# Gates of a GRU and an LSTM loop: input part seeded into PSUM, gates read one by one by ScalarE

## The reference, cut to what matters

```python
# GRU-like layer (h starts from cond_1024)
fused = sigmoid(concat([x_t, h]) @ w_W + w_b)
hidden_state, output_state = split(fused, 2)
memory_state = x_t @ wx_W + wx_b + hidden_state * (h @ wh_W + wh_b)
h_new = output_state * h + (1.0 - output_state) * tanh(memory_state)

# LSTM layer (c starts from 0, h from cond_1024)
a = (x_t @ Wx + b) + h @ Wh            # four parts i, f, o, g
next_c = sigmoid(f) * c + sigmoid(i) * tanh(g)
next_h = sigmoid(o) * tanh(next_c)
```

## Time and profile before

| | |
|---|---|
| median of 3 runs | 9069.2 us (9068.93 to 9073.12) |
| profiled execution, its own time | 9070.96 us |
| its span, first to last instruction | 9069.2 us |
| mean granted TensorE clock | 0.878 |
| PE / DVE / ACT / POOL busy | 73% / 83% / 48% / 17% of the span |
| `gru`, first to last product of the loop | 7719.5 to 8120.3 us |
| `lstm`, first to last product of the loop | 8425.8 to 8799.2 us |

### The profile page before, as it was taken

One profiled execution on the slowest core, in us unless ns is written; L12 is line 12 of the kernel. 1 busy time (PEld: TensorE's weight loads), 2 busy tenths in 40 slices (PEclk: granted clock), 3 DMA queues, 4 the chain that ended last, 5 costly groups with the idle time before them and its releaser, 6 DMA issues. The chain is left out here.

```text
span 9069.2 us, 110790 instructions
## 1 busy us (share of the span) xinstructions
PE 6612.7 (73%) x34945; PEld 2651.3 (29%) x35217; DVE 7509.4 (83%) x12442; ACT 4347.2 (48%) x4172; POOL 1508.4 (17%) x1495
## 2 busy tenths in 40 slices
PE   4777777777777777777777776288888887662779
PEld 1222323232323232323232322022222222331443
DVE  5899999999999999999999997799999998336223
ACT  3565656565656665666666564133333332112222
POOL 0000000000000000000000000177777775000000
PEclk7888888888888888888888887599999999996999
DMA  0000000000000000000000000000000000000000
GB/s 6 1 1 1 1 1 1 1 1 1 1 1 1 1 1 1 1 1 1 1 1 1 1 1 8 29 4 4 4 3 3 3 3 4 0 5 3 3 14 5
DMA packets 14004, 28.01 MB, mean 3 GB/s; under 512 B 3665, under 2 KB 11602, under 8 KB 12434
## 3 DMA queue, kind: packets, MB, share of 16 engines
q1 hardware_dynamic: 13586, 22.47, 0.9%
HBM read 15.12 MB, written 7.34 MB: 2 GB/s over the span
## 5 line engine op out<-in xcount | busy, mean ns | idle before, releaser
L897 POOL TENSOR_TENSOR hc<-hh,cg 128x512 f32<-128x512 f32 x1024 | 1294.4, 1267 | 513.4 <-DVE hh L880 513.4
L825 ACT ACTIVATE ps_m<-ps_m,aneg 128x508 f32<-128x508 f32 x1024 | 673.4, 658 | 1192.0 <-DVE hh L880 1067.7
L880 DVE TENSOR_TENSOR_SCAN hh<-ps_m,bx 128x512 f32<-128x512 f32 x1024 | 1236.1, 1212 | 0.0
L796 PE MATMUL ps_m<-hc,pick 128*128 128x512 f32 x2048 | 1053.1, 598 | 2.1 <-POOL hc L897 0.8
L507 DVE TENSOR_TENSOR_SCAN co<-rh_d 128x3088 f32<-128x3088 f32 x128 | 843.8, 6592 | 254.6 <-ACT rh_d L368 254.6
L230 POOL TENSOR_TENSOR t<-gs,minus 128x176 f32<-128x176 f32 x128 | 72.6, 567 | 5072.1 <-DVE gs L156 5072.1
L507 DVE TENSOR_TENSOR_SCAN co<-rx_d 128x772 f32<-128x772 f32 x544 | 915.4, 1746 | 0.0
L260 PE MATMUL r_ps<-rh_diag,whq 32*128 32x512 bf16 x3072 | 353.3, 624 | 767.6 <-DVE rh_diag L126 767.0
L862 DVE TENSOR_TENSOR bx<-ps_m,bg 128x512 f32<-128x512 f32 x1024 | 678.6, 668 | 50.3 <-PE ps_m L809 50.1
L252 PE MATMUL r_ps<-wdiag,xsp 32*128 32x512 bf16 x3312 | 348.5, 581 | 487.3 <-ACT rx_d L368 452.5
L398 ACT ACTIVATE rh_pd<-r_ps 128x512 f32<-128x512 f32 x512 | 264.6, 603 | 900.7 <-PE r_ps L260 900.7
(11 more groups left out here) (392 smaller groups left out, 11565.1 us busy)
## 6 DMA issues: line engine op xcount, KB each, us to landing
rows_scratch<-pc SPq DMA_DIRECT2D x48, 128.0 KB
rows<-rows_scratch SPq DMA_DIRECT2D x128, 48.0 KB
ew<-in_e SPq DMA_DIRECT2D x3, 1024.0 KB, 6.9
co<-in_x_dn SPq DMA_DIRECT2D x1, 1024.0 KB, 4.8
xcur<-in_x_dn SPq DMA_DIRECT2D x1, 1024.0 KB
out_x<-xcur SPq DMA_DIRECT2D x1, 1024.0 KB, 3.9
qi<-in_f_q SPq DMA_DIRECT2D x1, 384.0 KB, 3.1
xpw<-in_xp_t SPq DMA_DIRECT2D x1, 257.0 KB
```

The lines of the kernel that those rows point to most:

```text
L796: e.matmul(ps[:, 6, :], pick[:, 128 - un:256 - un], hc[un % NHC][:], start=False, stop=True, skip_group_check=True).then_inc(summed, 1)
L825: e.activation(da[un % NDA][:, :, 1:T], ps[:, un % 2, :].rearrange("p (n t) -> p n t", n=NG4)[:, :, 1:T], ACT.Exp, scale=aneg[:, 0:1]).the ...
L880: e.tensor_tensor_scan(hh[un % NBUF][:], da[un % NDA].rearrange("p n t -> p (n t)"), bx[un % NBUF][:], 0.0, ALU.mult, ALU.add).then_inc(sc ...
L897: e.tensor_tensor(hc[un % NHC][:], hh[un % NBUF][:], cg[:], ALU.mult).then_inc(weighted, 1)
```

## The change

TensorE gets the identity matrix `ident`. After the products of a step it executes seeds: it multiplies the identity by the next step's input part (`gx`) and so writes it into PSUM, in the other half of banks 0 to 5 (`at` is 0 or 3, changing every step). The products with the state then accumulate onto the seed (`start=False`). In `gru` there are two seeds per step (the two gates), in `lstm` three (input and forget gates together with 32 columns, the tanh gate, the output gate). `gx` is one step longer, with zeros behind the end, for the seed after the last step.

The addition on VectorE (L1024, L1106) is gone. TensorE signals `KP` = 3 times a step. ScalarE reads the gates from PSUM: in `gru` the reset gate after the first product, then after the third product the update gate and once more the same sum with scale -1 (`new`, one minus the gate); in `lstm` the pair of input and forget gates, then the tanh gate, then the output gate. In `gru` the order of the products is now reset, memory, update, and the end of a step is computed as h times gate (`old`), `new` times tanh, and their sum; three VectorE operations after tanh become two, since `old` does not need it. `WARM` goes from 6 to 3 in both loops.

```diff
--- before.py
+++ after.py
@@ -950,23 +950,23 @@
 
 
 STEPS = 16
-WARM = 6
-
-
-def gru(nc, xcur, gh, w):
+WARM = 3
+
+
+def gru(nc, ident, xcur, gh, w):
 
...
-        gx = sb("gx", [128, 3, COLS])
-        gate = sb("gate", [128, 2, N]); sg = sb("sg", [128, 2, N]); r1 = sb("r1", [128, N]); r2 = sb("r2", [128, N])
-        th = sb("th", [128, N]); r3 = sb("r3", [128, N]); r4 = sb("r4", [128, N])
+        gx = sb("gx", [128, 3, COLS + N])
+        reset = sb("reset", [128, N]); upd = sb("upd", [128, N]); new = sb("new", [128, N])
+        r1 = sb("r1", [128, N]); r2 = sb("r2", [128, N]); th = sb("th", [128, N]); old = sb("old", [128, N]); r4 = sb("r4", [128, N])
...
-        KV, KA = 6, 2
+        KV, KA, KP = 5, 4, 3
...
@@ -984,15 +984,23 @@
...
-                e.wait_ge(warm, 1)
+                e.wait_ge(warm, 2)
+
+                def seed(t, at):
+                    for q in range(2):
+                        e.matmul(ps[:, at + q, 0:N], ident[:], gx[:, q, bass.ds(N * t, N)], start=True, stop=True)
+
+                seed(0, 0)
                 with e.Fori(0, T // STEPS) as block:
                     for step in range(STEPS):
                         t = STEPS * block + step
+                        at = 3 * (step % 2)
                         e.wait_ge(vec, t * KV + 1)
                         h = gh[:, bass.ds(t, 1), :].rearrange("p a n -> p (a n)")
-                        for q in range(3):
-                            i = e.matmul(ps[:, q, 0:N], gw[:, 1, q * D:(q + 1) * D] if q < 2 else gwh[:], h, start=True, stop=True)
-                        i.then_inc(prod, 1)
+                        e.matmul(ps[:, at, 0:N], gw[:, 1, 0:D], h, start=False, stop=True, skip_group_check=True).then_inc(prod, 1)
+                        e.matmul(ps[:, at + 2, 0:N], gwh[:], h, start=True, stop=True).then_inc(prod, 1)
+                        e.matmul(ps[:, at + 1, 0:N], gw[:, 1, D:2 * D], h, start=False, stop=True, skip_group_check=True).then_inc(prod, 1)
+                        seed(t + 1, 3 - at)
                         for _ in range(WARM):
                             e.matmul(ps[:, 7, :], idle[:, 0:D], idle[:], start=True, stop=True)
 
@@ -1005,51 +1013,55 @@
                 with e.Fori(0, T // STEPS) as block:
                     for step in range(STEPS):
                         t = STEPS * block + step
-                        e.wait_ge(vec, t * KV + 2)
-                        e.activation(sg[:], gate[:], ACT.Sigmoid).then_inc(act, 1)
-                        e.wait_ge(vec, t * KV + 4)
+                        at = 3 * (step % 2)
+                        e.wait_ge(prod, t * KP + 1)
+                        e.activation(reset[:], ps[:, at, 0:N], ACT.Sigmoid).then_inc(act, 1)
+                        e.wait_ge(prod, t * KP + 3)
+                        e.activation(upd[:], ps[:, at + 1, 0:N], ACT.Sigmoid).then_inc(act, 1)
+                        e.activation(new[:], ps[:, at + 1, 0:N], ACT.Sigmoid, scale=-1.0).then_inc(act, 1)
+                        e.wait_ge(vec, t * KV + 3)
                         e.activation(th[:], r2[:], ACT.Tanh).then_inc(act, 1)
 
             @blk.vector
             def _(e):
                 e.memset(idle[:], 0.0).then_inc(warm, 1)
+                e.memset(gx[:, :, COLS:], 0.0).then_inc(warm, 1)
                 e.wait_ge(moved, 12)
                 e.memset(r1[:], 0.0).then_inc(vec, 1)
-                gxt = gx[:].rearrange("p q (t n) -> p t q n", n=N)
-                at = lambda x, t: x[:, bass.ds(t, 1)].rearrange("p a n -> p (a n)")
+                gxt = gx[:, 2, 0:COLS].rearrange("p (t n) -> p t n", n=N)
+                at_t = lambda x, t: x[:, bass.ds(t, 1)].rearrange("p a n -> p (a n)")
                 with e.Fori(0, T // STEPS) as block:
                     for step in range(STEPS):
                         t = STEPS * block + step
-                        e.wait_ge(prod, t + 1)
-                        e.tensor_tensor(gate[:], ps[:, 0:2, 0:N], gxt[:, bass.ds(t, 1), 0:2, :].rearrange("p a q n -> p (a q) n"),
-                                        ALU.add).then_inc(vec, 1)
+                        at = 3 * (step % 2)
+                        e.wait_ge(prod, t * KP + 2)
                         e.wait_ge(act, t * KA + 1)
-                        e.scalar_tensor_tensor(out=r1[:], in0=ps[:, 2, 0:N], scalar=gb[:, 3:4], in1=sg[:, 0, :],
+                        e.scalar_tensor_tensor(out=r1[:], in0=ps[:, at + 2, 0:N], scalar=gb[:, 3:4], in1=reset[:],
                                                op0=ALU.add, op1=ALU.mult).then_inc(vec, 1)
-                        e.wait_ge(vec, t * KV + 3)
-                        e.tensor_tensor(r2[:], r1[:], gxt[:, bass.ds(t, 1), 2, :].rearrange("p a n -> p (a n)"), ALU.add).then_inc(vec, 1)
+                        e.wait_ge(vec, t * KV + 2)
+                        e.tensor_tensor(r2[:], r1[:], at_t(gxt, t), ALU.add).then_inc(vec, 1)
                         e.wait_ge(act, t * KA + 2)
-                        e.tensor_tensor(r3[:], at(gh, t), th[:], ALU.subtract).then_inc(vec, 1)
+                        e.tensor_tensor(old[:], at_t(gh, t), upd[:], ALU.mult).then_inc(vec, 1)
+                        e.wait_ge(act, t * KA + 4)
+                        e.tensor_tensor(r4[:], new[:], th[:], ALU.mult).then_inc(vec, 1)
                         e.wait_ge(vec, t * KV + 5)
-                        e.tensor_tensor(r4[:], r3[:], sg[:, 1, :], ALU.mult).then_inc(vec, 1)
-                        e.wait_ge(vec, t * KV + 6)
-                        e.tensor_tensor(gh[:, bass.ds(t + 1, 1)].rearrange("p a n -> p (a n)"), r4[:], th[:], ALU.add).then_inc(vec, 1)
-
-
+                        e.tensor_tensor(at_t(gh, t + 1), r4[:], old[:], ALU.add).then_inc(vec, 1)
+
+
-def lstm(nc, xcur, lh, w):
+def lstm(nc, ident, xcur, lh, w):
...
-        KV, KA = 5, 3
+        KV, KA, KP = 4, 4, 3
@@ -1066,15 +1078,26 @@
                     e.matmul(ps[:, k % 8, :], lx[:, q * D:(q + 1) * D], xcur[:, c * 512:(c + 1) * 512], start=True, stop=True)\
                         .then_inc(parts, 1)
                 e.wait_ge(moved, 16)
-                e.wait_ge(warm, 1)
+                e.wait_ge(warm, 2)
+
+                def seed(t, at):
+                    for bank, q in ((0, slice(0, 2)), (1, slice(3, 4)), (2, slice(2, 3))):
+                        count = q.stop - q.start
+                        e.matmul(ps[:, at + bank, 0:count * N], ident[:], gx[:, q, bass.ds(N * t, N)], start=True, stop=True)
+
+                seed(0, 0)
                 with e.Fori(0, T // STEPS) as block:
                     for step in range(STEPS):
                         t = STEPS * block + step
+                        at = 3 * (step % 2)
                         e.wait_ge(vec, t * KV + 1)
                         h = lh[:, bass.ds(t, 1), :].rearrange("p a n -> p (a n)")
-                        for q in range(4):
-                            i = e.matmul(ps[:, q, 0:N], lwh[:, q * D:(q + 1) * D], h, start=True, stop=True)
-                        i.then_inc(prod, 1)
+                        for q, bank, lo in ((0, 0, 0), (1, 0, N), (3, 1, 0), (2, 2, 0)):
+                            i = e.matmul(ps[:, at + bank, lo:lo + N], lwh[:, q * D:(q + 1) * D], h, start=False, stop=True,
+                                         skip_group_check=True)
+                            if q:
+                                i.then_inc(prod, 1)
+                        seed(t + 1, 3 - at)
                         for _ in range(WARM):
                             e.matmul(ps[:, 7, :], idle[:, 0:D], idle[:], start=True, stop=True)
 
@@ -1087,32 +1110,33 @@
                 with e.Fori(0, T // STEPS) as block:
                     for step in range(STEPS):
                         t = STEPS * block + step
-                        e.wait_ge(vec, t * KV + 2)
-                        e.activation(s3[:], gate[:, 0:3, :], ACT.Sigmoid).then_inc(act, 1)
-                        e.activation(gg[:], gate[:, 3, :], ACT.Tanh).then_inc(act, 1)
-                        e.wait_ge(vec, t * KV + 5)
+                        at = 3 * (step % 2)
+                        e.wait_ge(prod, t * KP + 1)
+                        e.activation(keeps[:].rearrange("p a n -> p (a n)"), ps[:, at, 0:2 * N], ACT.Sigmoid).then_inc(act, 1)
+                        e.wait_ge(prod, t * KP + 2)
+                        e.activation(gg[:], ps[:, at + 1, 0:N], ACT.Tanh).then_inc(act, 1)
+                        e.wait_ge(prod, t * KP + 3)
+                        e.activation(out_[:], ps[:, at + 2, 0:N], ACT.Sigmoid).then_inc(act, 1)
+                        e.wait_ge(vec, t * KV + 4)
                         e.activation(tc_[:], cc[:], ACT.Tanh).then_inc(act, 1)
 
             @blk.vector
             def _(e):
                 e.memset(idle[:], 0.0).then_inc(warm, 1)
+                e.memset(gx[:, :, COLS:], 0.0).then_inc(warm, 1)
                 e.wait_ge(moved, 16)
                 e.memset(cc[:], 0.0).then_inc(vec, 1)
```

(23 more changed lines are left out.)

## The result

The changed kernel takes 9214.8 us (median of four runs, 9211.4 to 9223.5), the kernel before 9071.1 (four runs): ratio 1.016, 95% interval 1.014 to 1.018. It is slower by 144 us, where 185 were forecast (9254, range 9205 to 9345). The profiled execution took 9212.8 us, 141.9 more than that of before.

What follows compares the result with a forecast made beforehand. Before, the latency of each step's dependency chain bounded both loops; after, at 1.2 GHz, TensorE's queue would. GRU +28, LSTM +166, early full-clock steps -9: +185 us on 9071 gives 9256 profiled, 9254 as median; range 9205 to 9345.

Steps and rivals of the forecast that it cites:

- The step on which all turned: Both loops: three fills per step do not hold 2.4 GHz; the clock falls to 1.2 GHz within the first few steps.
- Rival A: Both loops: the clock stays at 1.00 because TensorE is hardly ever idle; 189 us faster, 8880 us; chance 0.10.
- TensorE's in-order queue bounds the step at the low clock: Both loops: products wait behind seeds and fills; steps of 3.36 us (GRU) and 4.22 us (LSTM), +28 and +166 us.
- Rival C: Both loops: clock falls but the state's dependency chain sets steps, 2.70 and 2.83 us; 9001 us; 0.03 including the page's load time.
- The low-clock steps: Steps at 1.2 GHz: 3.36 us in the GRU loop, 4.22 us in the LSTM loop.
- The gap behind the step's first pass: TensorE at 1.2 GHz, both loops: each small pass follows the one before by 0.215 us, the first included.
- The three fills: TensorE at 1.2 GHz, both loops: three 512-column fills at 0.43 us each, 1.29 us per step.
- the gap from the last seed to the first fill: TensorE at 1.2 GHz, both loops: taken as 0.13 us, against 0.11 at the full clock.
- The bounds that the prediction worked out: Total time: 33 us less without the 0.13 gap; 55 and 26 us more for later loads and register operations; 9221 to 9335.
- The steps at the full clock: Start of each loop: some three steps at 2.4 GHz before the clock falls, saving 1.1 (GRU) and 1.9 us (LSTM) each, -9 us.
- ScalarE's read of 128x16 from PSUM: Gate reads in both loops: 0.22 us taken, 0.27 as upper end, some 13 us over both loops.
- The price of the ring at the full clock: Product-to-product dependency chain at 2.4 GHz: 2.26 us per GRU step, 2.31 per LSTM step; 113 and 78 us less.

Runs made afterwards that it cites:

- e5: Kernel before the change, its data path untouched, with three fills per step instead of six (WARM 6 to 3): 9252.7 us, ratio 1.020.
- e2: Changed kernel with four fills per step instead of three (WARM 3 to 4): 9326.6 us in one run.
- e1: Changed kernel with no fills instead of three (WARM 3 to 0): 9008.0 us in one run.
- e8: Same as e7 but three fills instead of six, so one seed per gate for 16 steps: 9010.8 us in one run.
- e7: Changed kernel with one seed per gate for 16 steps instead of one per step, and six fills: 8872.3 us, ratio 0.978 to the kernel before.
- e4: Changed kernel with six fills per step instead of three, the number of the kernel before: 8945.0 us in one run.
- e3: Changed kernel with five fills per step instead of three: 8910.4 to 8914.6 us in four executions, 9211.9 in the traced one.
- e6: Changed kernel with five fills in the GRU loop and six in the LSTM loop instead of three: 8938.9 us, ratio 0.985 to the kernel before.

## Why the prediction was right, and where its sizes were off

The step on which all turned, that three fills do not hold the clock although TensorE is hardly ever idle, is shown from both sides: three and four fills, 0.50; six, 1.00; and by e5, where the fills alone were changed. The prediction argued it from the number of 512-column products in a stretch of another stage, in which TensorE had also stood idle for 2.1 us. The runs bear out the outcome. They vary only the number of fills, so that it is not shown that their columns are what counts. Rival A (8880 us) failed at the point named for it. The trace has the engine at 98 to 100 of 100 us with the clock at 0.50, so a rule of the clock by long idle gaps, as in the Trainium skill ("TensorE: Matmul & The Clock Gate", section "Why this matters for your kernels"), doesn't foretell this case; e5, with 27% idle, and e2, with none, have the same clock.

That TensorE's in-order queue bounds the step at the low clock is shown by the wait rows (3 of 127 steps waited for the state) and by e1, e2 and e8, where fills or seeds taken out of the queue shorten the step. Rival C, a step set by the ring, is refuted for three fills; in the GRU of e1, without fills, the ring does set the step, near the price that C had for it (2.65 us for 2.70).

The sizes:

- The low-clock steps were shorter than forecast: 3.23 us, not 3.36, in the GRU and 4.08, not 4.22, in the LSTM. Over some 122 low-clock steps of each loop this is about 33 of the 43 us between forecast (+185) and trace (+142). Three terms of the sum are off, read from the rows above. The gap behind the step's first pass was too large: I gave every pass 0.215 us. But in these steps the state is done before the last fill starts, and the first load of the next step runs under that fill (7905.77, where the product starts at 7906.19). The second pass then starts 0.07 us after the first (7906.26) and the second pair 0.29 us after it, not 0.43; in the LSTM the eight passes need 8604.50 - 8602.94 = 1.56 us, not 8 x 0.215 = 1.72. The three fills take 1.23 us (7904.96 to 7906.19), not 1.29. Against these, the gap from the last seed to the first fill was too small: four seed passes and this gap take 0.86 us (7904.10 to 7904.96), which is 4 x 0.215, so the gap is 0.215 and not 0.13.
- The bounds that the prediction worked out, 9221 to 9335, moved only the terms that could lengthen the step, and the 0.13. The measured 9214.8 lies below them, and within the stated range only by its widening to 9205; that part is luck.
- The steps at the full clock: three in the GRU, as forecast; in the LSTM 14 us, about six. The three more, at 1.9 us saved each, are some 6 us.
- ScalarE's read of 128x16 from PSUM took 0.18 us, below the 0.22 taken and the 0.27 held as the end. It changed nothing at the low clock, since the read isn't on TensorE's path.
- The price of the ring at the full clock held in the GRU: 2.22 us in its first steps and 2.28 on average in e7, for 2.26. In the LSTM 2.31 was too high: 2.16 us or less in the changed kernel, 2.19 in e7. There the state starts 1.87 us after the first product (8500.03 to 8501.90), not 1.99; the pair of gates is read at 0.64, not 0.74, and the product with the old cell starts 0.23 later, not 0.28. So the sentence that the ring would still bound both loops at the full clock fails for the LSTM: TensorE never waited for the state there, even with three fills. Rival A's 8880 was a fair price for the data path (e7: 8872), but only with six fills and without the seeds in every step's queue. With them the step is TensorE's, 2.33 and 2.77 (e4).

Not settled: which executions with five fills keep the clock in the LSTM loop. No run showed what differs at the loop's start. The clock fell within 2 us of it in the traces of e2, e3 and e6, and not in that of e4.

## What to carry to other kernels

Products that only keep TensorE's clock are part of the design of a latency-bound loop: change the loop's length or what else TensorE does, and their number must be measured again, on several executions, with the granted clock read for each loop by itself. The time is not monotonic in that number (9008, 9215, 9327, 8912 or 9212, 8945 us for 0, 3, 4, 5, 6), so one step up or down misleads. Once a fall at a loop's start has happened, it matters whether the loop brings the clock back: in e6 six fills did, in e3 five did not. When work is moved onto TensorE to shorten a chain, count its whole in-order queue against the new, shorter step, and move into the loop only what depends on the step: the same seeds done once for 16 steps were worth another 73 us.

## What was not expected of the hardware

With five fills the same kernel took 8910 to 8915 us in four executions and 9212 in a fifth. In the fifth, the one traced, the LSTM loop lost 2.4 GHz in its first 5 us, and TensorE busy at 80 of 80 us did not bring it back. With six fills a loop that had lost it in the same way had it back some 3 us later (e6). And the float32 weight load that opens a step is made under the last fill if the state is there in time (load at 7905.77, first pass at 7906.19, second at 7906.26): the first two pairs of passes then start 0.29 us apart at the low clock, the later ones 0.43. Where the state is late, the load waits for it like the product: at 7726.92, 0.28 us after the state's start at 7726.64 and 0.03 before the product, though no fill had started for 0.6 us.
